# Graph attention, four layers on one core: the last pass split by destinations, and the next layer begun before the maximum of all sources is known

## Time and profile before

| | us |
|---|---|
| median of 3 runs | 797.01 |
| lowest, highest | 794.25, 797.94 |
| the profiled execution | 794.59 |
| its span in the trace | 792.9 |
| PE busy in the span | 762.8 (96%) |
| DVE busy | 635.8 (80%) |
| ACT busy | 322.7 (41%) |

### The profile page before, as it was taken

How to read it: one execution, slowest core, us unless ns; L and a number is a source line. 1 busy time by engine, 2 the same in 40 slices (tenths; PEclk the granted TensorE clock), 3 DMA queues, 4 the chain that set the end, 5 groups by cost and what they waited for, 6 DMA issues and landing times. The chain is left out here.

```text
span 792.9 us, 16516 instructions
## 1 busy us (share of the span) xinstructions
PE 762.8 (96%) x6606; PEld 744.7 (94%) x6606; DVE 635.8 (80%) x1077; ACT 322.7 (41%) x847; POOL 16.1 (2%) x35
## 2 busy tenths in 40 slices
...
DMA packets 13852, 29.31 MB, mean 37 GB/s; under 512 B 1280, under 2 KB 7552, under 8 KB 13824
## 3 DMA queue, kind: packets, MB, share of 16 engines
...
## 5 line engine op out<-in xcount | busy, mean ns | idle before, releaser
L365 PE MATMUL acc<-V,probs 128*128 128x129 f32 x5632 | 639.9, 275 | 7.2 <-DVE probs L863 4.9
L365 PEld LDWEIGHTS acc<-V,probs 128*128 128x128 f32 x5632 | 634.8, 192 | 12.7 <-DVE probs L863 5.7
L863 DVE SCALAR_TENSOR_TENSOR probs<-rho,t_now,adjT 128x1024 f32<-128x1024 f32 x336 | 409.3, 1277 | 17.3 <-PE acc L365 11.5
L614 ACT ACTIVATE hpT<-rows 32x256 f32<-32x256 f32 x240 | 99.4, 414 | 76.2 <-DVE rows L900 73.5
L599 ACT ACTIVATE fill<-mean_now,empty 128x128 f32<-128x128 f32 x160 | 48.9, 394 | 88.0 <-DVE den L876 87.9
L908 DVE TENSOR_TENSOR X<-X,side 128x512 f32<-128x512 f32 x32 | 22.0, 688 | 69.4 <-PE side L389 69.4
L606 ACT ACTIVATE rows<-rows 128x512 f32<-128x512 f32 x44 | 27.7, 630 | 73.2 <-DVE rows L885 48.3
L885 DVE SCALAR_TENSOR_TENSOR rows<-acc,den,fill 128x128 f32<-128x128 f32 x160 | 43.9, 344 | 10.8 <-ACT fill L599 10.1
L550 ACT ACTIVATE V<-v_now 128x4 f32<-128x4 f32 x28 | 5.8, 209 | 80.6 <-PE side L300 80.6
L479 ACT ACTIVATE adjT<-stage 128x1024 bf16<-128x1024 int32 x32 | 33.1, 1053 | 7.6 <-DMA stage<-in_adj_t_dram 7.3
L389 PE MATMUL side<-Wout,hpT 128*128 (+1 forms) x256 | 31.4, 276 | 3.2 <-ACT hpT L614 3.0
...
## 6 DMA issues: line engine op xcount, KB each, us to landing
...
```

Source lines behind the costliest of these rows:

```text
L365: last = nc.tensor.matmul(group(c, k), probs[:, j % RING, k * P:(k + 1) * P], V[:, j, :], start=(j == 0 and k % PER_BANK == 0), stop=(j == ...
L614: last = nc.scalar.activation(hpT[b:b + Q, :, a:a + Q], rows[a:a + Q, 1, :, b:b + Q], ACT.Copy)
L863: nc.vector.scalar_tensor_tensor(probs[:, j % RING, :], rho[:, c * CH:(c + 1) * CH], t_now[:, j:j + 1], adjT[:, j, c * CH:(c + 1) * CH], A ...
```

## The change

Layers 1 to 3 are written anew, and the last unit of layer 0. A layer is now three passes p over the sources instead of two: p = 0 has the first 8 tiles of destinations (1024), p = 1 the next 6 (768), p = 2 the last 2 (256); pass 2 puts four blocks into one ring slot. The unit (0, 1) of layer 0 is passes 1 and 2 of "layer 0" in this numbering. What follows a pass runs beside the next one. The next layer's first 8 source tiles are set up during pass 1, with the maximum over these 8 only (`early_max`, `early_factors`). Its pass 0 begins with them; in its first 8 tiles the other 8 are set up; then the maximum over all is known, ACT multiplies the 8 groups accumulated so far in PSUM by a ratio per destination and the first 8 rows of V by one factor (`gaps`, `rest_factors`), and pass 0 goes on with tile 8. `divide` is gone in layers 1 to 3: ACT applies the nonlinear function straight from `acc` with the inverse denominator as its scale (`nonlinear_late`). The inverse root of the variance comes from Ln and Exp on ACT and one Newton step on DVE, instead of three steps on DVE. ELU's missing rows are added later (`mean_elu`, `add_fill`). The last head's blocks are transposed by PE instead of by DVE and ACT. The function table of ACT is loaded for GELU and back around each of the three passes of layer 1. `keep_warm` is gone from layers 1 to 3, and so is the loop over layers 2 and 3. The output is stored in three pieces. The core of the diff, indented less than in the file, blank lines left out:

```diff
...
+PARTS = (((0, 4), (4, 4)), ((0, 4), (4, 2)), ((6, 2),))
+FIRST, CHUNKS = (0, 2, 4), 5
+NORM_DVE = (3, 2, 1)
+HALF = NT // 2
...
+def slot_no(n, p, j):
+return NT * (2 * H - 2) + (2 * NT + NT // 4) * n + NT * p + (j // 4 if p == 2 else j)
...
+def late_unit(n, p, asides, first=0, end=NT):
+    c, v = half_of(p), V_of[n % 2]
+    for j in range(first, end):
+        if j == 0 and n == 0 and p == 1:
+            pe.wait_ge(rows_ready, 4 * H - 3)
+        if j == 0 and n > 0 and p == 0:
+            pe.wait_ge(early_v_ready, n)
+        if j == 0 and n > 0 and p == 1:
+            pe.wait_ge(all_v_ready, n)
+        if p == 0 and j >= HALF and j % 4 == 0:
+            pe.wait_ge(rest_v_ready, 2 * n - 1 + (j - HALF) // 4)
+        pe.wait_ge(probs_ready, tile_no(n, p, j) + 1)
+        for i, k in enumerate(groups(p)):
+            if p == 0 and j == HALF and k % PER_BANK == 0:
+                pe.wait_ge(bank_scaled, NB * (n - 1) + k // PER_BANK + 1)
+            last = nc.tensor.matmul(group(c, k), slot_of(n, p, j)[:, i * P:(i + 1) * P], v[:, j, :],
+                                    start=(j == 0 and k % PER_BANK == 0), stop=(j == NT - 1),
+                                    skip_group_check=True)
+            if p == 0 and j == HALF - 1 and k % PER_BANK == PER_BANK - 1:
+                last.then_inc(bank_summed, 1)
+            if k == groups(p)[-1]:
+                last.then_inc(summed, 1)
+            if i == len(groups(p)) // 2 - 1 and (j, 0) in asides:
+                asides[(j, 0)]()
+        if (j, 1) in asides:
+            asides[(j, 1)]()
...
+def early_scores(n, j):
+    return {(j, 0): lambda: late_wh(n, 0, 0), (j, 1): lambda: late_wh(n, 0, 1),
+            (j + 1, 0): lambda: late_s1(n, 0, hT_ready, chunk_no(n, 0, 0)),
+            (j + 1, 1): lambda: late_s1(n, 1, hT_ready, chunk_no(n, 0, 1)),
+            (j + 2, 0): lambda: max_rows(n, 0), (j + 3, 0): lambda: max_spread(n, 0)}
+late_unit(0, 1, {(2, 1): later_vectors,
+                 (4, 1): both(transpose_rows, (0, 0, x_added, 4 * H - 3), (0, 1, x_added, 4 * H - 3)),
+                 (6, 1): both(project_rows, (0, 0), (0, 1)),
+                 (11, 0): lambda: transpose_normed(1, 0, 0, x_written, chunk_no(1, 0, 0)),
+                 (11, 1): lambda: transpose_normed(1, 0, 1, x_written, chunk_no(1, 0, 1)),
+                 **early_scores(1, 12)})
+late_unit(0, 2, {})
+for n in range(1, 4):
+    scores_of_rest = {
+        (7, 1): lambda: (late_s1(n, 2, hT_ready, chunk_no(n, 2)), late_s1(n, 3, hT_ready, chunk_no(n, 2)))}
+    if n == 1:
+        asides = {(0, 1): both(transpose_rows, (1, 0, s1_kept, 1), (1, 1, s1_kept, 2)),
+                  (1, 1): both(project_rows, (1, 0), (1, 1)),
+                  (2, 1): lambda: transpose_rows(2, 0, x_written, chunk_no(1, 1, 1)),
+                  (3, 0): lambda: project_rows(2, 0),
+                  (4, 0): both(transpose_normed, (1, 1, 0, x_written, chunk_no(1, 1, 0)),
+                               (1, 1, 1, x_written, chunk_no(1, 2, 0))),
+                  (4, 1): both(late_wh, (1, 1, 0), (1, 1, 1)),
+                  (5, 1): lambda: transpose_normed(1, 2, 0, hT_ready, chunk_no(1, 1, 1)),
+                  (6, 0): lambda: late_wh(1, 2, 0),
+                  (6, 1): lambda: max_rows(1, 1), (7, 0): lambda: max_spread(1, 1)}
+    else:
+        asides = {(1, 1): both(transpose_normed, (n, 1, 0, s1_kept, 2 * n - 1), (n, 1, 1, s1_kept, 2 * n)),
+                  (2, 1): both(late_wh, (n, 1, 0), (n, 1, 1)),
+                  (4, 0): lambda: transpose_normed(n, 2, 0, hT_ready, chunk_no(n, 1, 1)),
+                  (4, 1): lambda: late_wh(n, 2, 0),
+                  (5, 1): lambda: max_rows(n, 1), (6, 1): lambda: max_spread(n, 1)}
+    late_unit(n, 0, {**asides, **scores_of_rest}, 0, HALF)
+    late_unit(n, 0, {} if n == 1 else
+              {(10, 1): lambda: mean_rows(n, WL[:, n - 1, 0:D], 1, late_r_ready, 6 * n)}, HALF, NT)
+    if n < 3:
+        bank_free = ((late_r_ready, 6) if n == 1 else (meanw_ready, n), (late_r_ready, 6 * n))
+        late_unit(n, 1, {(9, 1): lambda: transpose_normed(n + 1, 0, 0, *bank_free[0]),
+                         (10, 0): lambda: transpose_normed(n + 1, 0, 1, *bank_free[1]),
+                         **early_scores(n + 1, 11)})
+    else:
+        late_unit(n, 1, {})
+    late_unit(n, 2, {})
...
+def nonlinear_late(n, p):
+    c = half_of(p)
+    if n == 2:
+        nc.scalar.preload_act_table(ACT.Gelu)
+    act.wait_ge(late_rden, stage_no(n, p))
+    act.wait_ge(x_written, chunk_no(n, p, 0) - 1)
+    for first, count in PARTS[p]:
+        for k in range(first, first + count):
+            scale = late_den[:, c, 2, k:k + 1]
+            last = nc.scalar.activation(rows[:, 1, k, :], group(c, k)[:, 0:D], ACT.Gelu if n == 2 else ACT.Exp,
+                                        scale=scale)
+            if n > 2:
+                last = nc.scalar.activation(rows[:, 0, k, :], group(c, k)[:, 0:D], ACT.Relu, scale=scale)
+        last.then_inc(late_exp, 1)
+    if n == 2:
+        nc.scalar.preload_act_table_set(LOG_EXP)
...
+def early_factors(n):
+    act.wait_ge(late_d_ready, 2 * n - 1)
+    nc.scalar.activation(t_first[:, :], late_d[:, 0, 0:HALF], ACT.Exp, scale=1 - ALPHA).then_inc(t_first_ready, 1)
+    nc.scalar.activation(v_first[:, :], late_d[:, 0, 0:HALF], ACT.Exp, scale=ALPHA).then_inc(v_first_ready, 1)
+    late_rho(n, 0)
+    late_rho(n, 1)
+    v = V_of[n % 2]
+    act.wait_ge(v_first_ready, n)
+    nc.scalar.activation(v[:, 0:HALF, D], v_first[:, :], ACT.Copy)
+    for t in range(HALF):
+        last = nc.scalar.activation(v[:, t, 0:D], wh_at(t)[:, 0:D], ACT.Copy, scale=v_first[:, t:t + 1])
+    last.then_inc(early_v_ready, 1)
+def rest_factors(n):
+    v = V_of[n % 2]
+    act.wait_ge(late_d_ready, 2 * n)
+    nc.scalar.activation(t_now[:, :], late_d[:, 1, :], ACT.Exp, scale=1 - ALPHA).then_inc(t_rest_ready, 1)
+    nc.scalar.activation(v_now[:, HALF:NT], late_d[:, 1, HALF:NT], ACT.Exp, scale=ALPHA).then_inc(v_rest_ready, 1)
+    late_rho(n, 2)
+    late_rho(n, 3)
+    act.wait_ge(gap_ready, n)
+    nc.scalar.activation(ratio[:, :], gap[:, :], ACT.Exp).then_inc(ratio_ready, 1)
+    act.wait_ge(ratio_ready, n)
+    for b in range(NB):
+        if b < NB - 1:
+            act.wait_ge(bank_summed, (NB - 1) * (n - 1) + b + 1)
+        else:
+            act.wait_ge(summed, tile_no(n, 0, HALF))
+        for k in range(b * PER_BANK, min(NK, (b + 1) * PER_BANK)):
+            last = nc.scalar.activation(group(0, k), group(0, k), ACT.Copy, scale=ratio[:, k:k + 1])
+        last.then_inc(bank_scaled, 1)
+    act.wait_ge(v_rest_ready, n)
+    nc.scalar.activation(v[:, HALF:NT, D], v_now[:, HALF:NT], ACT.Copy)
+    for t in range(HALF, NT):
+        last = nc.scalar.activation(v[:, t, 0:D], wh_at(t)[:, 0:D], ACT.Copy, scale=v_now[:, t:t + 1])
+        if t % 4 == 3:
+            last.then_inc(rest_v_ready, 1)
+    late_rho(n, 4)
+    late_rho(n, 5)
+    nc.scalar.activation(v[:, 0:HALF, :], v[:, 0:HALF, :], ACT.Copy, scale=ratio[:, HALF:HALF + 1]).then_inc(all_v_ready, 1)
...
+late_fill_rows(0)
+late_exp_rows(0, 0)
+late_exp_rows(0, 1)
+late_copy_rows(0, 0)
+late_copy_rows(0, 1)
+for n in range(1, 4):
+    late_inverse_root(n, 0)
+    late_normed(n, 0)
+    late_relu(n, 0, 0)
+    late_relu(n, 0, 1)
+    keep_s1(n)
+    early_factors(n)
+    if n == 1:
+        late_fill_rows(1)
+        late_exp_rows(1, 0)
+        late_exp_rows(1, 1)
+        late_copy_rows(1, 0)
+        late_copy_rows(1, 1)
+        late_fill_rows(2)
+        late_exp_rows(2, 0)
+        late_inverse_root(n, 1)
+        late_normed(n, 1)
+        late_copy_rows(2, 0)
+    else:
+        nonlinear_late(n, 1)
+        late_inverse_root(n, 1)
+        late_normed(n, 1)
+        nonlinear_late(n, 2)
+    late_relu(n, 1, 0)
+    late_relu(n, 1, 1)
+    late_inverse_root(n, 2)
+    late_normed(n, 2)
+    late_relu(n, 2, 0)
+    rest_factors(n)
+    if n > 1:
+        late_mean(n)
+    nonlinear_late(n + 1, 0)
+nonlinear_late(4, 1)
+nonlinear_late(4, 2)
...
+def gaps(n):
+    peaks(n, 1)
+    nc.vector.tensor_tensor(gap[:, 0:HALF], peak[:, 0, :], peak[:, 1, :], ALU.subtract)
+    nc.vector.tensor_scalar(gap[:, HALF:HALF + 1], late_c[:, 0:1], late_c[:, 1:2], ALPHA, ALU.subtract,
+                            ALU.mult).then_inc(gap_ready, 1)
...
+def early_max(n):
+    take_scores(n, 0)
+    find_max(n, 0)
+    tiles(n - 1, 2, 0, 4)
+    max_of_row(n, 0)
+    tiles(n - 1, 2, 4, 6)
+    take_max(n, 0)
+    exponent_rows(n, 0)
+    exponent_rows(n, 1)
+    peaks(n, 0)
+    tiles(n - 1, 2, 6, 8)
+tiles(0, 1, 0, 8)
+late_denominators(1, 0)
+tiles(0, 1, 8, 9)
+late_divide(0, 0)
+tiles(0, 1, 9, 10)
+late_divide(0, 1)
+late_elu_rows(0, 0)
+tiles(0, 1, 10, 11)
+late_elu_rows(0, 1)
+tiles(0, 1, 11, 13)
+add_to_x(1, 0, 0)
+add_to_x(1, 0, 1)
+late_statistics(1, 0)
+tiles(0, 1, 13, 14)
+late_norm(1, 0)
+tiles(0, 1, 14, 16)
+early_max(1)
+late_denominators(1, 1)
+tiles(0, 2, 8, 16)
+late_divide(1, 0)
+late_divide(1, 1)
```

(95 more changed lines are left out.)

637 lines of the change are left out of this document (343 added, 294 removed).

## The result

The changed kernel takes 809.99 us (median of 4 runs, 806.76 to 811.05) against 795.63 (4 runs, 794.03 to 797.94): a ratio of 1.0171, interval 1.0129 to 1.0213. It is slower; the forecast was 808.0. The profiled execution has a span of 808.1 us (before 792.9) and a mean granted clock of 0.976 (before 0.994).

What follows compares the result with a forecast made beforehand. PE's stream of fp32 products was taken as the bound. 757.9 plus waits 44.7 gave 802.6; own time 1.7 more, 804.3; clock 1.4, 805.7; half the median's 2.4 excess and rounding, 808. Range 800 to 815, outer bounds 785 and 819.

Steps and rivals of the forecast that it cites:

- clock: After PE's long waits: of nine possible stretches at half clock costing 1.4 us each, only one was priced, 1.4 us.
- tail: After the last product: denominators, ACT and DVE operations, then 3.6 us from DMA issue to the end, 6.9 us in all.
- waits, unit (0, 1): Last unit of layer 0: PE waits 4.3 us at its transposes at (4, 1) and 1.0 at (11, 0).
- waits, layer 1, tiles 0 to 8: PE waits for DVE blocks queued behind round trips, then 3.9 us at tile 8; 19.0 us in sum.
- waits, layer 2, tiles 0 to 8: PE waits 2.7 us at (1, 1), 1.6 at (2, 1) and 3.1 at tile 8; 7.4 us in sum.
- wait at (9, 1) of layer 2: In pass 1 DVE is behind, so normalising ends at 706.5 while PE stands there since 700.8: 5.8 us.
- waits, layer 3, tiles 0 to 8: PE waits 4.2 us at (1, 1) and 3.0 at tile 8; 7.2 us in sum.
- The count of 757.9 us: Whole kernel's span if PE never waited: 513.7 start, 200.9 products, 36.4 set-up work, 6.9 tail.
- break-even of 35.0 us of waits: Sum of PE's new waits at which the change equals the kernel before: 792.9 - 757.9.
- Rival (b): Every PE wait past 2.7 us costs 1.4 us of clock, nothing hidden: 817 us, slower still; chance 0.16.
- the walk: From unit (0, 1) on, the queues of PE, DVE and ACT followed against each other: PE's new waits sum to 44.7 us.
- Rival (a): Waits overlap better; blocks 1 to 7 of layers 1 to 3 are ready when PE comes: 780 us, faster; chance 0.20.

Runs made afterwards that it cites:

- the filled kernel: The changed kernel with products of the identity into unread PSUM columns ahead of PE's long waits, nothing else changed: 797.45 us, ratio 1.0040 against before.
- the two other orders: On the changed kernel, each alone: denominators ahead of the fill in pass 1 of layers 2 and 3, 806.59 us; V for tiles 8 to 11 before the scalings, 805.42 us.
- the 786.52 of the table: The changed kernel with three reorderings (denominators early, layer 1 blocks one place earlier, V first) and identity products in the remaining waits: 786.52 us, ratio 0.9881 against before.

## Why the prediction came out right, step by step

The total is within 0.3% and the sign is right. That it is so close is luck: two large terms are off and cancel. Against the forecast's span of 804.0 the measured 808.1 has 9.5 us less of waits, 11.5 more of clock, 2.0 less of tail, 3.3 more of busy PE and small waits, and a head 0.8 longer, 4.1 more in sum; and the 2.3 us that the forecast added for the spread of the median and rounding were not needed.

| term | predicted | measured |
|---|---|---|
| waits, unit (0, 1) | 5.3 | 4.8 |
| waits, layer 1, tiles 0 to 8 | 19.0 | 15.3 |
| waits, layer 2, tiles 0 to 8 | 7.4 | 4.7 |
| wait at (9, 1) of layer 2 | 5.8 | 5.4 |
| waits, layer 3, tiles 0 to 8 | 7.2 | 5.1 |
| sum of waits | 44.7 | 35.2 |
| tail | 6.9 | 4.9 |
| clock | 1.4 | 12.9 |

- **Busy PE against gaps.** The count of 757.9 us plus waits, tail and clock gives the measured span to 3.3 us, once the head's 0.8 is taken off: 0.4 in smaller waits, and 2.9 by which PE's busy time in the stages above, 253.1, less the 12.9, exceeds the 237.3 of the count (200.9 + 36.4). Of these, 0.3 are in the count's own sum: its parts for the set-up work come to 36.7. The rest lies in the stages with many waits; from 601.99 to 651.61, with none, the count's parts give 48.0 and the clock 1.7, and PE was busy 49.62. Each wait cuts the stream, and the last instruction ahead of it is recorded with its full 0.28 us instead of 0.112: 16 x 0.17 = 2.7, an estimate that no run tests. The break-even of 35.0 us of waits was the right way to put the question, and the waits measured 35.2. Without the clock the change is worth nothing: the filled kernel is 3.6 us over before.
- **The clock is the step that failed**, in "Price nothing to 9 x 1.4 = 12.6; ... so I take one, 1.4". PE lost 12.9 us in seven stretches and 12.0 came back when its waits were filled; almost nothing was hidden by the waits that follow. Rival (b) was right in its cause, though its 817 stood on the too long waits. That its 12.6 is near 12.9 is chance: it has nine falls at 1.4, and there were seven at 1.4 to 2.9. Its price was cut short as well, for the stretch of the earlier trace rows goes on in the next microsecond of the kernel before, and in full costs 1.7:

```profile
28.00:29.00 1.00, 1.00 (x9) 1.00 (x8) 1.00 (x2) 1.00 (x2) 0.00 (x0) 0.72 0.80 283
```

The reason against it, that ahead of layer 1 PE was idle in pieces at clock 1.00, was read from the kernel with fillers; the same kernel without them goes to 0.53 there.
- **The waits were 9.5 us too long.** They stood where the walk put them, and almost all at the engine that it named:

```profile
525.10 0.63 PE L461 MATMUL side<-ident,rows 128*128 128x128 f32 x4 [2.55 <-DVE rows L1220]
527.10 0.83 PE L461 MATMUL side<-ident,rows 128*128 128x128 f32 x4 [1.36 <-DVE rows L1220]
527.73 4.32 PE L442 MATMUL acc<-V,probs 128*128 128x129 f32 x24
```

```profile
657.00 0.85 PE L482 MATMUL side<-ident,xn 128*128 128x128 f32 x6 [1.66 <-ACT xn L836]
...
660.85 1.61 PE L491 MATMUL acc<-WL,hT 128*128 128x130 f32 x12 [1.21 <-ACT hT L845]
...
676.25 7.27 PE L442 MATMUL acc<-V,probs 128*128 128x129 f32 x48 [1.86 <-ACT V L899]
...
711.43 1.09 PE L482 MATMUL side<-ident,xn 128*128 128x128 f32 x4 [5.36 <-ACT xn L836]
...
740.39 0.85 PE L482 MATMUL side<-ident,xn 128*128 128x128 f32 x6 [3.25 <-ACT xn L836]
...
758.17 2.19 PE L442 MATMUL acc<-stage,probs 128*128 128x129 f32 x14 [1.87 <-ACT stage L899]
```

At (4, 1) the walk had 4.3 and 2.55 + 1.36 are seen; the 24 instructions behind them take 4.32 us instead of 24 x 0.112 = 2.7, over half of them at half clock. At (9, 1) it had 5.8, measured 5.36, for the reason given. At (2, 1) of layer 2 it had 1.6 against 1.21, at (1, 1) of layers 2 and 3 2.7 and 4.2 against 1.66 and 3.25, and at tile 8 3.9, 3.1 and 3.0 against 2.77, 1.86 and 1.87. PE's own slow pace covers a part of a wait that follows (sixteen instructions of 3.81 us at tile 1 leave less to wait for at tile 2), but at most 1.0 us in all: of 13.0 lost, 12.0 came back.
- **Unit prices,** busy time over count, from the groups by shape:

```profile
L1172 DVE SCALAR_TENSOR_TENSOR probs<-rho,t_now,adjT 128x768 f32<-128x768 f32 x61 | 59.0, 1008 | 4.1 <-PE acc L442 2.5 <-PE acc L418 1.5
...
L1172 DVE SCALAR_TENSOR_TENSOR probs<-rho,t_now,adjT 128x256 f32<-128x256 f32 x64 | 26.3, 475 | 0.1
...
L916 ACT ACTIVATE fill<-mean_w,minus_one,empty 128x128 f32<-128x128 f32 x32 | 12.8, 481 | 3.8 <-DVE X L1337 2.6 <-DVE mean_w L1331 1.2
...
L894 ACT ACTIVATE acc<-acc,ratio 128x129 f32<-128x129 f32 x24 | 6.5, 360 | 0.1
...
L874 ACT ACTIVATE V<-acc,v_first 128x128 f32<-128x128 f32 x8 | 2.2, 377 | 0.0
```

A block of 768 takes 59.0/61 = 0.97 (0.95 by the line), one of 256 26.3/64 = 0.41 (0.41). The scaling inside PSUM takes 6.5/24 = 0.27, below the 0.31 that was its lower bound, and so does a column of V from PSUM (2.2/8); the 8 scalings take 2.0 us instead of 2.5 and the column and four rows of V behind them 1.35 instead of 1.5, 0.7 of the 1.1 by which tile 8's wait in layer 1 is shorter than forecast. The fill on ACT takes 12.8/32 = 0.40, against the 0.31 for 128 columns.
- **The tail** is 2.0 us shorter:

```profile
803.22 0.16 DVE L1190 COPY late_den<-acc 128x2 f32<-128x2 f32 x1 [1.30 <-PE acc L442]
...
805.44 0.43 DVE L1239 TENSOR_TENSOR X<-X,rows 128x256 f32<-128x256 f32 x1
805.90 0.37 SPq L302 DMA_DIRECT2D out_dram<-X  x1
```

The chain up to the last add, at 805.87, takes 2.7 us where 3.2 were counted, and from there to the end it is 2.2 us instead of 3.6: the forecast took the time of the transfer in the earlier trace rows, which has 512 KB, for one of 128 KB. From issue to landing these take 3.2 and 1.8 us by the DMA view.
- **Landmarks.** The first product of layer 2 was forecast for 645.5 and comes at 651.6, of layer 3 for 726 and 733.4, the last for 796 and 803.2: they are 6.1 to 7.4 us late, and ahead of the first of them 7.7 us are lost to the clock.
- **Rival (a)** needed blocks 1 to 7 ready. They are not in this order. With DVE one block ahead, blocks 2, 4, 5 and 6 are, and the waits of layer 1 fall from 15.3 to 9.2 us; with the two other orders and the fillers the kernel is the 786.52 of the table. The idea wins 1.2%; the order in which DVE and ACT took their turns and the missing fillers lost 2.9%.
